# A two-layer graph network on one core: node stages over more beats, own-row products split from the sums, a shorter last set, padding chunks left out

## The reference

```python
# 6250 nodes, 100000 edges sorted by dst, D = 128
def _layer(h, edge_feats, src, dst, deg, iso, Wn, Ws, Wi, num_nodes):
    msg = (h[src] + edge_feats) @ Wn.T
    agg = jax.ops.segment_sum(msg, dst, num_segments=num_nodes)
    agg = agg / jnp.maximum(deg, 1.0)[:, None]
    self_msg = jnp.where(iso[:, None], h @ Wi.T, h @ Ws.T)
    x = agg + self_msg
    return jnp.where(x >= 0, x, RRELU_SLOPE * x)

deg = segment_sum(ones, dst);  iso = deg == 0
h = _layer(x, edge_attr, src, dst, deg, iso, Wn0, Ws0, Wi0, 6250)
h = _layer(h, edge_attr, src, dst, deg, iso, Wn1, Ws1, Wi1, 6250)
return _layernorm(x + h)
```

## Time and profile before

| | |
|---|---|
| median of 3 runs | 1106.08 us (1105.55 to 1108.45) |
| the profiled execution | 1106.56 us, its span 1104.8 us |
| busy share of the span | PE 87%, PEld 81%, DVE 63%, ACT 48%, POOL 69% |
| instructions in the trace | 38550 |
| mean granted TensorE clock | 0.955 of full speed |

### The profile page before, as it was taken

The page is one execution under the profiler, slowest core; times in us unless marked ns, Lnnn a source line. Parts: engine busy times, 40 slices in busy tenths (PEclk is TensorE's granted clock), DMA queues, the critical chain, the costliest instruction groups (busy, mean ns, idle before and its releaser), DMA issues. The chain is left out here.

```text
span 1104.8 us, 38550 instructions
## 1 busy us (share of the span) xinstructions
PE 961.7 (87%) x14625; PEld 900.1 (81%) x14625; DVE 690.5 (63%) x2323; ACT 530.1 (48%) x1211; POOL 760.8 (69%) x761
## 2 busy tenths in 40 slices
PE   1599989899999898998988997579999999999982
PEld 0488878788888888887878886479999999999982
DVE  7888877898888887886788875303233322423333
ACT  6487776777787777786777773100000000000000
POOL 8367766777747777656777657077777777777772
PEclk9999998999999998998999998689999999999996
DMA  9577886788778787787778888799988888898742
GB/s 296 162 220 277 277 284 223 252 296 272 241 265 258 234 299 235 239 290 240 224 241 274 267 279 253 231 369 280 272 264 268 277 264 266 265 273 277 208 117 53
DMA packets 154761, 278.42 MB, mean 252 GB/s; under 512 B 21538, under 2 KB 113228, under 8 KB 150604
## 3 DMA queue, kind: packets, MB, share of 16 engines
q1 hardware_dynamic: 93776, 184.33, 50.0%
q0 software_dynamic: 35776, 73.32, 23.3%
q10 hardware_dynamic: 25020, 18.25, 5.2%
HBM read 203.24 MB, written 72.57 MB: 250 GB/s over the span
## 5 line engine op out<-in xcount | busy, mean ns | idle before, releaser
L474 POOL DMA_INDIRECT rows<-x_parts_rows,idx x444 | 453.5, 1021 | 200.5 <-issue 124.0
L980 ACT CAST counts<-ps_count 128x294 f32 x992 | 438.3, 504 | 152.5 <-PE ps_count L1187 65.8
L474 POOL DMA_INDIRECT rows<-h_parts_rows,idx x288 | 277.5, 963 | 116.3 <-issue 82.0
L1199 PE MATMUL ps_dense<-counts,h_parts 128*128 128x144 bf16 x2940 | 322.8, 228 | 5.5 <-DVE sums L716 4.4
L1187 PE MATMUL ps_count<-is_code,is_lane 128*128 128x294 bf16 x992 | 301.6, 310 | 26.0 <-ACT counts L980 23.9
L1199 PE MATMUL ps_count<-counts,h_parts 128*128 128x144 bf16 x4557 | 300.6, 228 | 6.7 <-DMA counts<-counts_kept 6.7
L1199 PEld LDWEIGHTS ps_count<-counts,h_parts 128*128 128x128 bf16 x4557 | 290.5, 99 | 7.2 <-DMA counts<-counts_kept 7.0
L1138 PE MATMUL ps_win<-onehot,feats 128*128 128x40 f32 (+1 forms) x1568 | 246.0, 236 | 31.4 <-DVE sums L694 24.7
L1199 PEld LDWEIGHTS ps_dense<-counts,h_parts 128*128 128x128 bf16 x2940 | 215.7, 98 | 42.0 <-ACT counts L980 5.3
L1138 PEld LDWEIGHTS ps_win<-onehot,feats 128*128 128x128 f32 (+1 forms) x1568 | 208.9, 159 | 38.6 <-issue 30.9
L683 DVE TENSOR_SCALAR is_code<-codes,code 128x637 bf16<-128x637 f16 x496 | 197.7, 399 | 0.0
(11 more groups left out here) (97 smaller groups left out, 843.0 us busy)
## 6 DMA issues: line engine op xcount, KB each, us to landing
counts_kept<-counts SPq DMA_DIRECT2D x31, 1764.0 KB
counts<-counts_kept SPq DMA_DIRECT2D x217, 252.0 KB
feats<-in_edges_dram SPq DMA_DIRECT2D x196, 256.0 KB
rows<-x_parts_rows,idx POOLq DMA_INDIRECT x444
h_parts_rows<-row_parts ACTq DMA_DIRECT2D x17, 288.0 KB
x_parts_rows<-h_parts SPq DMA_DIRECT2D x7, 672.0 KB
h_parts<-h_parts_rows SPq DMA_DIRECT2D x7, 672.0 KB, 9.2
rows<-h_parts_rows,idx POOLq DMA_INDIRECT x288
```

The source lines that it names most:

```text
L474: nc.gpsimd.indirect_dma_start(rows[:, SUB * slot + c, :], None, table[:, :], bass.IndirectOffsetOnAxis(ap=indices[:, c:c + 1], axis=0)).t ...
L980: nc.scalar.copy(counts[:, j % BUFFERS, :, at(offset + first, count)], ps_count[:, q % BANKS, 0:count * TILES].rearrange("p (r t) -> p t r ...
L1199: last = nc.tensor.matmul(bank, h_parts[:, t, k, :], counts[:, b, t, :], start=(t == 0 and k == 0), stop=(t == TILES - 1 and k == PARTS - 1))
```

## The change

- **Beats of layer 0.** A table `STAGE` replaces the fixed offsets. For sets 0 to 14 (`SLOW`): activate stays at +4, `cut_h` moves to +5, its last third becomes `last_part` at +6, keep_h moves to +6, keep_turned to +7. For sets 15 and 16 (`FAST`) the whole stage takes four beats.
- **`SPLIT`** is chosen so that DVE cuts no features in a beat with inputs, activate or parts; there are 78 such windows as before.
- **Products.** `node_products` becomes `self_products` (own rows, into `ps_self`, counted by `self_out`) and `sum_products` (`ps_node`, `node_out`). ACT copies `ps_self` to SBUF (`keep_self`) in place of scaling; DVE multiplies and adds tile by tile with `scalar_tensor_tensor`, three instructions of 128 columns in place of one of 384.
- **Layer 1** (`LATER`): inputs at -2, own-row products and keep_self at -1, products with the sums at +1, activate at +2, normalize at +3.
- **Last set**: two tiles instead of three in every step. **Padding**: the last window has two chunks instead of four, in both layers.

```diff
+    SLOW = {"inputs": 0, "degrees": 1, "invert": 2, "products": 3, "activate": 4, "parts": 5, "last_part": 6,
+            "turn": 5, "keep": 6, "keep_turned": 7}
+    FAST = {"inputs": 0, "degrees": 1, "invert": 1, "products": 2, "activate": 2, "parts": 3, "last_part": 3,
+            "turn": 3, "keep": 3, "keep_turned": 4}
+    STAGE = {(0, name, READY[0][u] + (FAST if u >= TRIOS - 2 else SLOW)[name]): u
+             for u in range(TRIOS) for name in SLOW}
+    LATER = {"inputs": -2, "self": -1, "products": 1, "activate": 2, "normalize": 3}
+    STAGE.update({(1, name, max(READY[1][u] + after, 0)): u for u in range(TRIOS) for name, after in LATER.items()})
...
+    SPLIT, share = [], 0.0
+    for k in range(WINDOWS):
+        share += SPLIT_RATE
+        if share >= 1 and all((0, name, k - 2) not in STAGE for name in ("inputs", "activate", "parts")):
+            SPLIT.append(k)
+            share -= 1
...
+        def chunks_in(n):
+            return min(SUB, REAL_CHUNKS - chunk_of(n))
+        def real(u):
+            return 3 if u < TRIOS - 1 else TILES + 1 - 3 * u
...
             def activate(layer, u):
-                dve.wait_ge(mean_made, 3 * (n + 1))
-                nc.vector.tensor_tensor(total[:, :], ps_self[:, 0, 0:TRIO], mean[:, :],
-                                        ALU.add).then_inc(total_made, 1)
+                dve.wait_ge(node_out, n + 1)
+                dve.wait_ge(self_kept, n + 1)
...
+                for t in range(real(u)):
+                    d = slice(t * D, (t + 1) * D)
+                    nc.vector.scalar_tensor_tensor(total[:, d], ps_node[:, 0, d], deg_inv[:, u, t:t + 1],
+                                                   self_sums[:, d], ALU.mult, ALU.add).then_inc(total_made, 1)
...
+            def last_part(u):
+                dve.wait_ge(h_rest_made, u + 1)
+                if u:
+                    dve.wait_ge(parts_stored, 16 * u)
...
-            def scale(layer, u):
+            def keep_self(layer, u):
...
+                act.wait_ge(self_out, n + 1)
+                nc.scalar.copy(self_sums[:, c], ps_self[:, 0, c]).then_inc(self_kept, 1)
...
             def layer1():
                 for k in range(BEATS[1]):
-                    node_stage(1, k)
+                    if (1, "self", k) in STAGE:
+                        u = STAGE[1, "self", k]
+                        keep_self(1, u)
+                        if u + 1 < TRIOS:
+                            load_next(u + 1)
+                    if (1, "normalize", k) in STAGE:
+                        u = STAGE[1, "normalize", k]
+                        root(u)
+                        if u + 1 < TRIOS:
+                            load_next_x(u + 1)
+                        store_any(u)
...
+            def self_products(layer, u):
+                pe.wait_ge(node_in, n + 1)
+                for t in range(real(u)):
+                    for k, left in ((1, h_con), (2, h_in)):
+                        last = nc.tensor.matmul(ps_self[:, 0, t * D:(t + 1) * D], left[:, t * P:(t + 1) * P],
+                                                wts[:, k, :], start=k == 1, stop=k == 2)
+                last.then_inc(self_out, 1)
...
+            def sum_products(layer, u):
+                if layer:
+                    pe.wait_ge(sums_ready, u + 1)
+                for t in range(real(u)):
+                    last = nc.tensor.matmul(ps_node[:, 0, t * D:(t + 1) * D], sums[:, SUM, at(u * TRIO + t * P, P)],
+                                            wts[:, 0, :], start=True, stop=True)
+                last.then_inc(node_out, 1)
```

More of the change, by code:

```diff
@@ L325, in chunk_of, with rows_of @@
             return g * GC + SUB * j
+        def chunks_in(n):
+            return min(SUB, REAL_CHUNKS - chunk_of(n))
+        def rows_of(r):
+            return 16 * sum(chunks_in(GATHERED[i]) for i in range(r % ROWS, r + 1, ROWS))
         def dense_bank(nth):
@@ L796, in normalize @@
                 dve.wait_ge(rstd_made, u + 1)
[L797 to L798 removed]
+                dve.wait_ge(mv_made, total_count(u))
+                for t in range(real(u)):
                     r = res[:, t * D:(t + 1) * D]
@@ L801, in normalize, with node_stage0, node_stage1 @@
                                             ALU.subtract, ALU.mult).then_inc(y_made, 1)
[L803 to L821 removed]
+            def node_stage0(beat):
+                if (0, "last_part", beat) in STAGE and (0, "parts", beat) not in STAGE:
+                    last_part(STAGE[0, "last_part", beat])
+                if (0, "invert", beat) in STAGE:
+                    invert(STAGE[0, "invert", beat])
+                if (0, "activate", beat) in STAGE:
+                    activate(0, STAGE[0, "activate", beat])
+                if (0, "parts", beat) in STAGE:
+                    cut_h(STAGE[0, "parts", beat])
+                    if (0, "last_part", beat) in STAGE:
+                        last_part(STAGE[0, "last_part", beat])
+                if (0, "inputs", beat) in STAGE:
+                    node_inputs(0, STAGE[0, "inputs", beat])
+            def node_stage1(beat):
+                if (1, "activate", beat) in STAGE:
+                    activate(1, STAGE[1, "activate", beat])
+                    statistics(STAGE[1, "activate", beat])
+                if (1, "normalize", beat) in STAGE:
+                    normalize(STAGE[1, "normalize", beat])
+                if (1, "inputs", beat) in STAGE:
+                    node_inputs(1, STAGE[1, "inputs", beat])
             def layer0():
@@ L886, in node_trio @@
                     cut_h(u)
+                    last_part(u)
                 else:
@@ L1263, in turn @@
                     pe.wait_ge(turned_kept, u)
-                for t in range(3):
+                for t in range(real(u)):
                     last = nc.tensor.transpose(ps_node[:, 0, t * P:(t + 1) * P],
@@ L1267, in turn, with node_early0 @@
                 last.then_inc(h_turned, 1)
-            def node_early(layer, beat):
-                for u in range(TRIOS):
-                    k = node_at(layer, u, beat)
-                    if layer == 0 and k == 1:
-                        turn_degrees(u)
-                    if k == (1 if layer else 3):
-                        node_products(layer, u)
+            def node_early0(beat):
+                if (0, "degrees", beat) in STAGE:
+                    turn_degrees(STAGE[0, "degrees", beat])
+                if (0, "products", beat) in STAGE:
+                    self_products(0, STAGE[0, "products", beat])
+                    sum_products(0, STAGE[0, "products", beat])
             def node_late(beat):
-                for u in range(TRIOS):
-                    if node_at(0, u, beat) == 5:
-                        turn(u)
+                if (0, "turn", beat) in STAGE:
+                    turn(STAGE[0, "turn", beat])
             def layer0():
```

245 lines of the change are left out of this document (110 added, 135 removed).

## The result

The changed kernel takes 1087.27 us (median of 4 runs, 1085.4 to 1090.34) against 1105.82 us before (4 runs), a ratio of 0.9835 with a 95% interval of 0.9802 to 0.9867. Timed once more later, it stood at 0.9868 (0.9836 to 0.9901). The forecast was 1084.0 us.

A forecast was written before the change was run, and what follows sets the result against it. Layer 0 was taken as bound by PE, held by DVE or ACT, and layer 1 by POOL. 1106.56 - 14 (layer 0) - 5.3 (turn) - 2.8 (layer 1) - 0.5 (tail) = 1084.0 us, own range 1071 to 1094 us.

The forecast's parts named there:

- Layer 0 (-14): Sets 0 to 14: spreading DVE's bursts saves 9 us of DVE's gaps, 2 of ACT's and 3 of half clock.
- ACT term: Layer 0: of 10.9 us of PE's gaps that end with ACT, 2 us go, as scaling becomes one copy.
- PE's idle time above 45 us: Sign for layer 0: the forecast is wrong if PE's idle time there stays above 45 us.
- The DVE term: Layer 0: of 13.7 us of PE's gaps behind DVE's bursts, two thirds go, 9 us.
- rival (a): Layer 0: bunching isn't what holds PE, gaps move to other beats, layer 0 stays; 1098 us, chance 0.16.
- The half clock: Layer 0: a quarter of 12 us is gained from stretches at half clock, 3 us.
- The turn (-5.3): Between the layers: set 16's inputs start sooner, the store goes at 706.3 us, POOL starts 5.3 us sooner.
- Rival (c): Turn: loads and stores meet on shared DMA engines, POOL starts only 2 us sooner; 1087 us, chance 0.10.
- Rival (d): Layer 0: ACT stops in keep_h for `last_part`, 1.3 us in each of 15 sets; slower, 1117 us, chance 0.08.
- Two gathers: Layer 1: two gathers fall away at the end, 2.8 us sooner.
- The tail: After the last window: set 15's store at +3.9 us, set 16's statistics wait for its landing; 0.5 us sooner.
- PE is as full: Layer 1: bound by POOL, with PE as full, 69.1 of 70 us busy.

The follow-up runs named there:

- e_burst: The changed kernel with DVE's five instructions of sets 0 to 14 back in one beat and ACT's copies one beat sooner: 1092.52 us, 0.9855 of the kernel before.
- e_mid15: The changed kernel with set 15's products, activation and parts back where they stood before: 1089.68 us, 0.9853 of the kernel before.
- e_keep: The changed kernel with ACT's copies of the parts and transposed columns of sets 0 to 14 one beat later: 1096.17 us, 0.9918 of the kernel before.
- e_burst_tail_cols: The changed kernel with set 16's inputs and own-row products a beat sooner, window columns loaded 4 at a time, DVE's burst and ACT's copies as before: 1072.39 us, 0.9691.
- e_cols: The changed kernel with DVE's registers for layer 0's window columns loaded 4 at a time instead of 7: 1079.44 us, 0.9739 of the kernel before.
- e_split: The changed kernel with the old list of windows whose features are cut, two of every five: 1088.90 us, 0.9828 of the kernel before.
- e_hold: The changed kernel with SP's loads of the parts held until the last set's store has landed: 1087.14 us, 0.9828 of the kernel before.
- e_pad: The changed kernel with the two padding chunks gathered and multiplied again in each layer's last window: 1091.49 us, 0.9885 of the kernel before.

## Why the prediction was right, point by point

**Layer 0 (-14) failed by half, in its ACT term.** "Of ACT's 10.9 us I take 2 us": PE's waits for ACT grew by 9.3 us instead, and e_burst, with the copies of the parts back a beat, takes 9.4 us away again. By the prediction's own sign (PE's idle time above 45 us) this step was wrong: PE's gaps over 0.25 us between 60 and 690 us sum to 49.5 us, after 53.0. The DVE term held. The waits for DVE's sums fell by 12.5 us where 9 were taken, and 8.8 of these away from the register loads. Of the 13.7 us that the prediction counted behind the bursts, 2.8 end with the sum of a window that begins a load; the gap that it set apart, "2.23 us at 165.52 in a beat with no stage near", is a load, with DVE idle for 3.86 us ahead of that window's sum. So in what it came to, the spreading went as rival (a) has it: the gaps moved, from DVE to ACT, and the two pairs of runs show no gain of the spreading as such, and a loss of about 3 us by the medians once the loads are short.

The half clock fell by 17 us where 3 us of gain were taken; PE's busy time up to the last sum is 5.0 us shorter in this pair of profiles. That is less than it differs between profiles of the changed layer 0 (569 to 577 us), so it can be chance. What the remaining gain of layer 0 comes from (2 to 7 us, as the totals or the profile have it; PE's gaps account for some 4) stays open: the scaling that became one copy and the products in two steps were not tried apart.

**The turn (-5.3) was right in its chain, but for a tie, and mis-sized in one term.** The landing of a store was taken as at most 8.2 us; it took 6.9 for set 15's (e_mid15) and 6.8 for the last. The first makes the store 1.2 us sooner, the second POOL's start 1.4: together the 2.6 us that were missed. In the changed kernel the landing (about 696.75, 6.88 us after 689.87) and `h_diff` (696.79) come together, so `row_parts` is just about not what binds. In e_keep, e_burst_tail_cols, e_cols and e_split it does, as the prediction had it: there ACT's copy waits for the landing, 6.1, 7.0, 7.2 and 8.1 us after the issue. Setting set 15 ahead is worth 3.2 us of the 7.9 (e_mid15); the rest, the two tiles and the copy in place of the scaling above all, was not tried apart.

**Rival (c) had the right mechanism and the wrong outcome.** Loads beside it do hold a store back: 2.83 us without SP's loads, 6.82 beside them (e_hold). The Trainium skill (Trainium Kernel Development and Optimization, Key Constraints) says that transfers of all the queues interleave on the same 16 engines; the trace agrees with that. The Trainium skill's fit (DMA: Bandwidth & Descriptors, Anatomy of one DMA), made for the gpsimd path, gives about 2.45 us for 192 KB as an estimate. This store, on ACT's queue, released POOL 0.4 us later than that without the loads, and 4.4 later beside them. But POOL came sooner, not later: set 16's store released it after 6.8 us where 8.2 were taken. Whether that is because it is a third smaller isn't shown, since set 15's store of three tiles took 6.9 (e_mid15). Rival (c)'s total, 1087 us, is the measured one by accident: its layer 0 was 6.7 us too good and its POOL 5.9 us too late.

**Rival (d) came true in small.** ACT is held for the last part twice, 2.7 us in all, not in every set; what cost more was the new place of ACT's copies.

**Layer 1 and the tail.** Two gathers: -2.4 in this pair of profiles, 2.5 within e_pad's (forecast -2.8). Not foreseen: the last window is done sooner after the last gather, with half as many products, -1.3 us. The tail went step by step as written; set 15's store took 4.15 us to release DVE, within the 3.1 to 5.0 assumed. The estimate of 2.4 us that the prediction took from the Trainium skill's fit falls short of it. "PE is as full" was read too strictly: e_hold shows room.

## What to carry to other kernels

Before putting gaps down to the work that stands next to them, look at the same kind of gap where that work is missing: here more than half of PE's waits for DVE stood at register loads, and four registers at a time in place of seven gave 9 us, more than all of the spreading. Spreading one engine's burst moves what another engine does with the results; price the new meetings there too. And where runs differ by several us through one stage, cut the span at fixed events and compare pieces: the tail was plain there and hardly to be seen in the total. Know how far such a piece differs without any edit, too: two gathers (2.5 us) are less than the 2.8 us by which the time of 286 gathers differs from profile to profile. The kernel with the lowest ratio here, e_burst_tail_cols (0.9691), keeps the burst.

## What the runs showed of the hardware that was not expected

The time of a register load on DVE is not proportional to its count: in e_cols four values took 0.34 us in 38 of 49 loads, in the changed kernel seven took 1.6 us in 15 of 28 and 3.7 to 4.7 in seven. These seven stand at the same windows (35, 42, 91, 140, 154, 182, 189) as in the kernel before, where they take 3.0 to 5.5 us (DVE idle for 3.86 us up to 165.13 and 3.81 up to 568.94). Why these seven are so long isn't known.

A store of 192 KB released its waiter after 2.83 us without SP's loads beside it (e_hold), and after 6.6 to 7.2 us beside them in the changed kernel and its other variants. In the changed kernel the DMA engines have a busy share of 1.10 by the profile's count, that is, they are full, from 697.8 to 704.6 us.
